# Value products for four units in a row with eight buffers of probabilities, and two steps between a copy and the product that needs it in both halves

## The chip, the cores and the metric

The kernel runs on one core of one Trainium2 chip. The metric is the device time of one launch in microseconds (us). The kernel before took 1185.13 us, the median of three runs (1181.31, 1185.13 and 1186.98).

## The reference

One decoder layer on 64 sequences of 128 tokens with 128 features: self-attention with 16 heads of width 8, cross-attention of the same form on 77 context tokens with a mask, and a mixture of 8 experts of which each token takes 2. In front of each stands a layer norm, behind each a residual sum.

```python
q = x @ Wq.T * (1.0 / sqrt(D));  k = x @ Wk.T;  v = x @ Wv.T          # (B, S, 16, 8) each
attn = softmax(einsum('bqhd,bkhd->bhqk', q, k));  out = einsum('bhqk,bkhd->bqhd', attn, v) @ Wff.T + bff
...
scores = einsum('bhqd,bhkd->bhqk', q, k) / sqrt(8);  scores = where(mask == 0, -1e9, scores)
...
gate_scores = einsum('bsd,ed->bse', l2norm(x @ Wp.T), l2norm(sim_matrix)) / temperature
top_v, top_i = top_k(gate_scores, 2);  comb = sum(one_hot(top_i, E) * softmax(top_v)[..., None], -2)
h = gelu(einsum('bsd,edf->ebsf', x, W1) + b1);  out = einsum('ebsd,bse->bsd', h @ W2 + b2, comb)
...
x = x + attn(layernorm(x));  x = x + xattn(layernorm(x), ctx);  x = x + ffn(layernorm(x))
```

## The kernel before, in words

The program has two phases. Phase A (to about 860 us) does both attentions, the gate and the sorting of tokens by expert. Phase B (from about 880 us) runs the experts over tiles of 512 tokens. The change lies in phase A alone.

Phase A works on blocks of four sequences, 16 in all. Its outer loop counts t from -3 to 19 (`steps`), and each engine has its own copy of the loop body. Each body has two halves. The x half attends block t ("s", self-attention) and at the same time forms the maxima for block t+1 ("m"). The y half attends the context for block t-2 ("c") and forms the maxima for block t-1 ("cm"). Everything else (transposes, projections, layer norms, the gate) belongs to blocks t-3 to t+3 and is hung between the units of these two halves.

One half has 16 units (one sequence, four heads) and 19 steps, u = 0 to 18. In step u TensorE does, in this order: `scores` of unit u (four products into one of two banks `sc_m`, in the y half also the mask's product), `shifted` of unit u-1 (the same products, less the maxima, into one of two banks `sc_a`), in some steps `values` (the products of probabilities and values), and then what `in_x` or `in_y` names for that step. Before `scores(u)` it waits for the maximum of unit u-2, before `shifted(u)` for the exponential of unit u-2, since each has two banks. VectorE takes the maximum of each unit (`maxima`, a reduction) and then what its own `in_x` or `in_y` names for the step. ScalarE takes the exponential of unit u-1 (`attend`) into `probs` and then what its tables name. All three engines work through their instructions in the order in which the code lists them.

`values` of one unit are four products of fp32 numbers with 32 columns of weights each, which stand beside each other in the array (`pv[...][VW * c:VW * (c + 1)]`). An fp32 product is two matmuls in the trace, so a unit has 8 of them. All other products have 128 or 77 columns of weights. Before, `values` of two units follow in steps 4, 6, 8, ... 18:

```python
if u >= LEAD + 2 and u % 2 == 0:
    values(n, b, u - LEAD - 3, va, last)
    values(n, b, u - LEAD - 2, va, last)
```

GpSimd splits maxima and remainders and issues the sorted stores. The Sync queue carries nearly all DMAs in the order of its code: in the y half it stores the split q, k and ck of the coming blocks (each waits for GpSimd), then loads `xin`, the x of block t+3, then stacks q and k. `stats("1", t + 3, xin)` on VectorE is the only reader that waits for this load; it starts the layer norm ("1") of block t+3, which ScalarE's `normalise` finishes in the next x half.

Of the kernel before, what the change touches and what calls it, by code (L numbers as in the profile page):

```python
# [33 lines left out]
NS = 4  # L34
# [33 lines left out]
NO = NS // 2  # L68

# [12 lines left out]
def program(nc, x, ctx_in, mask, Wq, Wk, Wv, Wff, bff, xWq, xbq, xWk, xbk, xWv, xbv, xWo, xbo,  # L82
            Wp, WpT, sim, temp, W1, b1, W2, b2, out):
    ctx = ExitStack()
    with ctx:
# [63 lines left out]
        xn = {n: sa(f"xn_{n}", [128, NS, D]) for n in ("1", "2")}  # L149
# [21 lines left out]
        probs = [sa(f"probs{i}", [128, T]) for i in range(4)]  # L171
# [126 lines left out]
        with nc.Block() as block:  # L298
# [277 lines left out]
            def _(act):  # L576
# [50 lines left out]
                def body(t, par):  # L627
                    def in_x(u):
# [13 lines left out]
                        if u == 8 and on_(t + 2):  # L642
                            evac(xnT["1"][:], "x1T", t + 2, 0)
                        if u == 9 and on_(t):
                            evac(cT[:], "cT", t, 1, TC)
                        if u == 10 and on_(t + 2):
                            first("q", t + 2)
                        if u == 11 and on_(t):
                            wait_block(act, dumped["ck"], t - 1)
                            first("ck", t, bk_c)  # L650
                        if u == 12 and on_(t + 2):
                            second("q", t + 2)
                        if u == 13 and on_(t + 2):
                            first("k", t + 2)
                        if u == 13 and on_(t):
                            second("ck", t)

                    def in_y(u):
# [12 lines left out]
                        if u in (8, 9) and on_(t - 3):  # L671
                            half = u - 8
# [10 lines left out]
                        if 10 <= u < 10 + NS and on_(t):  # L683
                            normalise("2", t, x2, u - 10)
# [30 lines left out]
            def _(dve):  # L715
# [68 lines left out]
                def choose(b):  # L784
# [8 lines left out]
                    for s in range(NS):  # L793
# [4 lines left out]
                        .then_inc(dv_ok.sem, 1)  # L798
                    for s in range(NS):
# [48 lines left out]
                def body(t, par):  # L848
                    def in_x(u):
                        if u < NO and on_(t - 3):  # L850
                            divide("c", t - 3, u)
                        if u == 6 and on_(t - 3):
                            wait_block(dve, x3_st, t - 4)
                            add_residual("c", t - 3, x2res[1 - par], x3)
                        if u == 7 and on_(t - 3):
                            stats("3", t - 3, x3)
                        if u == 11 and on_(t + 2):
                            wait_block(dve, part3["cq"], t - 1)
                            remainder("q", t + 2)
                        if u == 12 and on_(t):  # L860
                            wait_block(dve, part3["ck"], t - 1)
                            remainder("ck", t, bk_c)
                        if u == 14 and on_(t + 2):
# [710 lines left out]
```

## Time and profile before

| | |
|---|---|
| median of three runs | 1185.13 us (1181.31 to 1186.98) |
| the profiled execution | 1185.62 us, of which its span is 1183.9 us |
| PE busy | 996.1 us (84% of the span) |
| ACT, DVE, POOL busy | 799.0, 749.3, 593.3 us |
| granted TensorE clock, mean | 0.941 |

PE is TensorE's matmuls, PEld its weight loads, DVE is VectorE, ACT ScalarE, POOL GpSimd, SPq the Sync queue. A line of the timeline merges neighbouring instructions of one group: its first number is the start of the first, its second the time from there to the end of the last. Matmuls overlap in the trace, so what a group costs is the time from its start to the start of the next group, not its duration.

### The profile page before, as it was taken

To read this page: it belongs to the slowest core of one execution; us is meant where nothing else is said; L and a number is where in the kernel's file an instruction comes from. 1 tells how busy PE (TensorE), PEld (TensorE's weight loads), DVE (VectorE), ACT (ScalarE), POOL (GpSimd) and SP (SyncE) were. 2 spreads that over 40 slices of the span, in tenths; PEclk is the share of its full clock that TensorE was granted. 3 is DMA by queue.
4 is the path that set the end of the run, shared out by engine and by line. 5 is a ranking of instruction groups with operands and counts; after the bars stand their busy time and mean duration, and the time that the engine had idled before them with its cause. 6 is when DMAs were issued, how large, how long until landed. Compare 5 with 4: busy or idle time off the path is not lost. (4 is left out here: it accounts for less than half of the span.)

```text
span 1183.9 us, 31785 instructions
## 1 busy us (share of the span) xinstructions
PE 996.1 (84%) x11621; PEld 767.5 (65%) x11621; DVE 749.3 (63%) x2074; ACT 799.0 (67%) x1649; POOL 593.3 (50%) x821
## 2 busy tenths in 40 slices
PE   2567889999999999999999999847529999999940
PEld 1345667777777777777777777635418888888830
DVE  2554746666667666676666674423258888888836
ACT  2144557777777777777777777635419999999930
POOL 4313423365655664664654643544534666666650
PEclk9997999999999999999999999978759999999975
DMA  3337684455455555545545642230452444232319
GB/s 92 83 75 157 141 187 102 120 142 146 128 151 134 134 136 140 142 126 140 151 112 147 147 110 73 57 81 31 136 161 76 125 129 113 79 83 75 84 56 372
DMA packets 120387, 144.16 MB, mean 122 GB/s; under 512 B 34189, under 2 KB 98528, under 8 KB 115432
## 3 DMA queue, kind: packets, MB, share of 16 engines
q1 hardware_dynamic: 108888, 120.33, 40.0%
q0 software_dynamic: 9168, 17.21, 4.8%
q10 hardware_dynamic: 2176, 4.59, 1.0%
q8 instruction: 93, 1.52, 0.6%
q14 instruction: 62, 0.51, 0.1%
HBM read 88.38 MB, written 55.36 MB: 121 GB/s over the span
## 5 line engine op out<-in xcount | busy, mean ns | idle before, releaser
L615 ACT ACTIVATE probs<-sc_a 77x512 f32<-77x512 f32 (+1 forms) x512 | 301.0, 592 | 148.5 <-PE sc_a L1008 93.2
L757 DVE TENSOR_REDUCE negm_m<-sc_m 128x4 f32<-128x512 f32 x256 | 169.5, 683 | 82.5 <-PE sc_m L987 81.4
L1305 POOL DMA_INDIRECT y_d<-yo,row x156 | 160.7, 1030 | 115.0 <-DVE yo L1419 73.6
L757 DVE TENSOR_REDUCE negm_cm<-sc_m 128x4 f32<-128x308 f32 x256 | 119.1, 471 | 144.5 <-PE sc_m L992 143.0
L477 POOL DMA_INDIRECT xs_d<-xrow,slot_i x128 | 131.9, 1031 | 121.3 <-PE sc_a L1008 80.0
L1022 PE MATMUL pv<-probs,big 128*32 128x128 f32 x4096 | 165.7, 280 | 0.6
L987 PE MATMUL sc_m<-ks,qs 96*128 96x128 bf16 x1024 | 105.3, 230 | 37.5 <-DMA ks<-stk_k 13.4
L1022 PEld LDWEIGHTS pv<-probs,big 128*32 128x32 f32 x4096 | 96.3, 109 | 56.2 <-ACT probs L615 28.6
L1400 DVE TENSOR_TENSOR gl<-g,gh 128x512 fp32r<-128x512 f32 x156 | 107.4, 689 | 35.1 <-ACT g L1349 34.6
L987 PEld LDWEIGHTS sc_m<-ks,qs 96*128 96x128 bf16 x1024 | 71.6, 102 | 82.6 <-issue 55.8
L1003 PE MATMUL sc_a<-cqs,cks 102*77 102x128 bf16 x1024 | 102.0, 223 | 4.9 <-DMA cqs<-cmscr 4.8
L1003 PE MATMUL sc_a<-qs,ks 102*128 102x128 bf16 x1024 | 101.1, 223 | 1.2 <-ACT probs L615 1.2
L1008 PE MATMUL sc_a<-identb,mbias 128*77 128x512 bf16 x256 | 99.9, 390 | 0.0
L987 PE MATMUL sc_m<-cks,cqs 96*128 96x77 bf16 x1024 | 80.6, 202 | 20.9 <-DMA cqs<-cmscr 16.4
L1003 PEld LDWEIGHTS sc_a<-cqs,cks 102*77 102x77 bf16 x1024 | 89.1, 119 | 12.7 <-issue 6.0
L987 PEld LDWEIGHTS sc_m<-cks,cqs 96*128 96x128 bf16 x1024 | 65.5, 100 | 41.6 <-issue 27.3
L992 PE MATMUL sc_m<-mbias,identb 128*128 128x308 bf16 x256 | 78.7, 308 | 0.0
L1003 PEld LDWEIGHTS sc_a<-qs,ks 102*128 102x128 bf16 x1024 | 69.5, 99 | 5.1 <-ACT probs L615 2.5
L454 POOL TENSOR_TENSOR xres<-xagain,bff_b 128x512 f32<-128x512 f32 x16 | 20.4, 1272 | 96.5 <-DMA xagain<-x_dram 96.5
L1524 PE MATMUL pv<-gl,vh 128*128 128x512 f32 x156 | 64.7, 415 | 0.0
L1518 PE MATMUL pv<-gh,vh 128*128 128x512 f32 x156 | 62.4, 400 | 0.0
L1519 PE MATMUL pv<-gh,vl 128*128 128x512 f32 x156 | 61.8, 396 | 0.0
(202 smaller groups left out, 2333.7 us busy)
## 6 DMA issues: line engine op xcount, KB each, us to landing
xg<-xs_d SPq DMA_DIRECT2D x39, 260.0 KB
stk_q<-parts_q SPq DMA_DIRECT2D x16, 384.0 KB, 2.9
stk_k<-parts_k SPq DMA_DIRECT2D x16, 384.0 KB, 2.7
qs<-stk_q SPq DMA_DIRECT2D x16, 384.0 KB, 5.9
ks<-stk_k SPq DMA_DIRECT2D x32, 192.0 KB
stk_cq<-parts_cq SPq DMA_DIRECT2D x16, 384.0 KB, 2.9
cqs<-stk_cq SPq DMA_DIRECT2D x16, 384.0 KB
xin<-x_dram SPq DMA_DIRECT2D x16, 256.0 KB
```

Source lines behind the costliest of these rows:

```text
L477: nc.gpsimd.indirect_dma_start(out=xs_d, in_=xrow[b % 2][:, c // 2, c % 2, :], in_offset=None, out_offset=bass.IndirectOffsetOnAxis(ap=slo ...
L615: nc.scalar.activation(probs[e % 4][0:rows], sc_a[e % 2][0:rows], ACT.Exp, scale=scale)\
L757: nc.vector.tensor_reduce(out=negm[n][:, s, HG * g + 4 * half:HG * g + 4 * half + 4], in_=sc_m[u % 2][:, 0:4 * cols].rearrange("p (j k) -> ...
L987: i = nc.tensor.matmul(sc_m[u % 2][:, j * cols:(j + 1) * cols], qst[0:KR, 4 * half + j, s * S:(s + 1) * S], kst[0:KR, HG * g + 4 * half + ...
L992: i = nc.tensor.matmul(sc_m[u % 2][:, 0:4 * cols], identb[:], bias[:, s, :].unsqueeze(1).broadcast_to([128, 4, cols]), start=False, stop=T ...
L1003: i = nc.tensor.matmul(sc_a[u % 2][0:cols, j * S:(j + 1) * S], kst[:, HG * g + 4 * half + j, s * cols:(s + 1) * cols], qst[:, 4 * half + j ...
L1008: i = nc.tensor.matmul(sc_a[u % 2][0:cols, :], bias[:, s, :], identb[:].unsqueeze(1).broadcast_to([128, 4, S]), start=False, stop=True, sk ...
L1022: i = nc.tensor.matmul(pv[s // 2][VW * c:VW * (c + 1), slot * S:(slot + 1) * S], va[:, HG * s + 4 * half + c, g, :], probs[u % 4][:, c * S ...
L1305: nc.gpsimd.indirect_dma_start(out=y12_d, in_=yo[par][:, c, :], in_offset=None, bounds_check=2 * B * S - 1, oob_is_err=False, out_offset=b ...
L1400: nc.vector.tensor_tensor(out=gl[c][:], in0=g[c][:], in1=hi32(gh[c][:]), op=ALU.subtract).then_inc(gl_ok.sem, 1)
L1518: nc.tensor.matmul(o, vh[par][:, w], gh[c][:], start=(c == 0), stop=False)
L1524: nc.tensor.matmul(y_banks[par][:], vh[par][:, c * 128:(c + 1) * 128], gl[c][:], start=False, stop=(c == FC - 1)).then_inc(w2_done.sem, 1)
```

## The change

`values` now follow for four units in steps 6, 10, 14 and 18, and `probs` has eight buffers in place of four. To make room the layer norms "1" and "2" share one buffer `xn`. Many entries of the tables move by one step, so that two steps lie between a copy on ScalarE and the product that reads it. One entry moves further: `stats("1", t + 3, xin)` on VectorE goes from step 10 of the y half to step 5. The gate's `choose` is cut in two (`choose`, `point`).

```diff
+NP = 8
-        xn = {n: sa(f"xn_{n}", [128, NS, D]) for n in ("1", "2")}
+        xn = dict.fromkeys("12", sa("xn", [128, NS, D]))
-        probs = [sa(f"probs{i}", [128, T]) for i in range(4)]
+        probs = [sa(f"probs{i}", [128, T]) for i in range(NP)]
...
@@ ScalarE, attend @@
-                            if e >= 4:
-                                act.wait_ge(pv_ok[n].sem, pv_ok[n].val(b, e - 3))
-                            nc.scalar.activation(probs[e % 4][0:rows], sc_a[e % 2][0:rows], ACT.Exp, scale=scale)\
+                            if e >= NP:
+                                act.wait_ge(pv_ok[n].sem, pv_ok[n].val(b, e - NP + 1))
+                            nc.scalar.activation(probs[e % NP][0:rows], sc_a[e % 2][0:rows], ACT.Exp, scale=scale)\
@@ ScalarE, in_x: x1T 8 to 9, cT 9 to 10, q 10 to 11, ck 11 to 12, second q 12 to 13 @@
-                        if u == 13 and on_(t + 2):
+                        if u == 14 and on_(t + 2):
                             first("k", t + 2)
-                        if u == 13 and on_(t):
+                        if u == 14 and on_(t):
                             second("ck", t)
@@ ScalarE, in_y: the gate's copies 8, 9 to 9, 10; normalise "2" 10..13 to 11..14 @@
...
@@ VectorE, in_x: add_residual c 6 to 7, stats 3 7 to 8, remainders q, ck, k one later @@
@@ VectorE, in_y @@
-                        if u == 6 and on_(t):
+                        if u == 5 and on_(t + 3):
+                            dve.wait_ge(x_in.sem, x_in.val(t + 3))
+                            stats("1", t + 3, xin)
+                        if u == 7 and on_(t):
                             wait_block(dve, x2res_ok, t - 1)
                             add_residual("s", t, xres, x2)
-                        if u == 7 and on_(t):
+                        if u == 8 and on_(t):
                             stats("2", t, x2)
-                        if u == 10 and on_(t + 3):
-                            dve.wait_ge(x_in.sem, x_in.val(t + 3))
-                            stats("1", t + 3, xin)
                         if u == 12 and on_(t - 3):
                             choose(t - 3)
                         if u == 13 and on_(t - 3):
+                            point(t - 3)
+                        if u == 14 and on_(t - 3):
                             mark(t - 3)
...
@@ TensorE, values and beside @@
-                                             probs[u % 4][:, c * S:(c + 1) * S], start=(g == 0), stop=(g == 1))
+                                             probs[u % NP][:, c * S:(c + 1) * S], start=(g == 0), stop=(g == 1))
...
-                            if u >= LEAD + 2 and u % 2 == 0:
-                                values(n, b, u - LEAD - 3, va, last)
-                                values(n, b, u - LEAD - 2, va, last)
+                            if u >= 6 and u % 4 == 2:
+                                for v in range(u - 6, u - 2):
+                                    values(n, b, v, va, last)
@@ TensorE, in_x: project c 5 to 6, x1T, cT, q, ck one later @@
-                        if u == 13 and on_(t + 2):
+                        if u == 14 and on_(t + 2):
                             product("k", t + 2, w_k[:], xnT["1"][:], T)
@@ TensorE, in_y: project s 5 to 6, the gate's products 8, 9 to 9, 10, x2T, rank, cq one later @@
```

The order on TensorE from step 5 of the y half of a full block on, before. `pv<-probs` are the value products (line 1022), `sc_m` and `sc_a` those of `scores` and `shifted`, `w_ff` the projection and `third_m` the transposed maxima:

```order
L987 MATMUL sc_m<-cks,cqs 128x77 x4
L992 MATMUL sc_m<-mbias,identb 128x308
L1003 MATMUL sc_a<-cqs,cks 77x128 x4
L1008 MATMUL sc_a<-identb,mbias 77x512
L1022 MATMUL pv<-probs,big 32x128 x8
L1046 MATMUL wb<-identb,third_m 48x128 x4
```

And in the changed kernel, where the same places have the lines 993, 998, 1009, 1014, 1028, 983 and 1052:

```order
L993 MATMUL sc_m<-cks,cqs 128x77 x4
L998 MATMUL sc_m<-mbias,identb 128x308
L1009 MATMUL sc_a<-cqs,cks 77x128 x4
L1014 MATMUL sc_a<-identb,mbias 77x512
L1028 MATMUL pv<-probs,big 32x128 x16
L983 MATMUL wb<-w_ff,onT 128x128 x4
L1052 MATMUL wb<-identb,third_m 48x128 x4
```

The groups of value products are twice as long and half as many, and the projection has moved behind one of them.

The order on VectorE in the y half of the same block, before. `negm_cm` are the maxima, `lnst<-xin` is the layer norm of the load, `x<-wb,xres` the residual sum:

```order
L757 TENSOR_REDUCE negm_cm<-sc_m 128x4 x5
L780 TENSOR_TENSOR x<-wb,xres 128x512
L757 TENSOR_REDUCE negm_cm<-sc_m 128x4
L731 BN_STATS lnst<-x 128x6 x4
L736 BN_AGGR lnmv<-lnst 128x2 x4
L757 TENSOR_REDUCE negm_cm<-sc_m 128x4 x3
L731 BN_STATS lnst<-xin 128x6 x4
L736 BN_AGGR lnmv<-lnst 128x2 x4
L757 TENSOR_REDUCE negm_cm<-sc_m 128x4 x2
```

And in the changed kernel (lines 758, 732, 737 and 781):

```order
L758 TENSOR_REDUCE negm_cm<-sc_m 128x4 x4
L732 BN_STATS lnst<-xin 128x6 x4
L737 BN_AGGR lnmv<-lnst 128x2 x4
L758 TENSOR_REDUCE negm_cm<-sc_m 128x4 x2
L781 TENSOR_TENSOR x<-wb,xres 128x512
L758 TENSOR_REDUCE negm_cm<-sc_m 128x4
L732 BN_STATS lnst<-x 128x6 x4
L737 BN_AGGR lnmv<-lnst 128x2 x4
L758 TENSOR_REDUCE negm_cm<-sc_m 128x4 x4
```

The statistics of `xin` now stand behind the sixth reduction (two stand ahead of these rows), in front of the residual sum; they stood behind the eleventh.

The order on ScalarE at the end of the x half, before. `parts_k<-wb` copies the product k, `probs` are the exponentials:

```order
L597 ACTIVATE parts_q<-rest_q 128x512
L615 ACTIVATE probs<-sc_a 128x512
L590 ACTIVATE parts_k<-wb 128x512
L597 ACTIVATE parts_ck<-rest_ck 128x308
L615 ACTIVATE probs<-sc_a 128x512 x3
L625 ACTIVATE oT<-pv 128x512
```

And in the changed kernel (lines 598, 616, 591 and 626):

```order
L598 ACTIVATE parts_q<-rest_q 128x512
L616 ACTIVATE probs<-sc_a 128x512
L591 ACTIVATE parts_k<-wb 128x512
L598 ACTIVATE parts_ck<-rest_ck 128x308
L616 ACTIVATE probs<-sc_a 128x512 x2
L626 ACTIVATE oT<-pv 128x512
```

The copy of k now has two exponentials behind it in its half in place of three.

## Rows read from the trace of the kernel before

**Rows 1.** Stretches: us, busy (instructions) of PE PEld DVE ACT POOL, PEclk, DMA share, GB/s.

```profile
250.00:700.00 450.00, 437.65 (x6476) 335.51 (x6476) 298.57 (x942) 338.96 (x756) 260.22 (x398) 1.00 0.54 137
```

**Rows 2.** Waits of PE from 250 to 700 us: total, times, longest.

```profile
PE sc_m L987 <- DVE negm_m L757: 7.6, 11, 0.7
```

**Rows 3.** Timeline of PE, one x half (start, us, what): value groups and neighbours.

```profile
425.82 0.39 PE L1003 MATMUL sc_a<-qs,ks 102*128 102x128 bf16 x4
426.05 0.39 PE L987 MATMUL sc_m<-ks,qs 96*128 96x128 bf16 x4
...
432.26 0.39 PE L1003 MATMUL sc_a<-qs,ks 102*128 102x128 bf16 x4
432.57 0.64 PE L1022 MATMUL pv<-probs,big 128*32 128x128 f32 x16
433.15 0.40 PE L987 MATMUL sc_m<-ks,qs 96*128 96x128 bf16 x4
```

**Rows 4.** Timeline of PE cut at 426.9 us, which leaves 12 matmuls.

```profile
426.59 0.53 PE L1022 MATMUL pv<-probs,big 128*32 128x128 f32 x12
```

**Rows 5.** Timeline of PE, fourth step of the same x half.

```profile
419.36 0.40 PE L987 MATMUL sc_m<-ks,qs 96*128 96x128 bf16 x4 [0.70 <-DVE negm_m L757]
```

**Rows 6.** Timeline of DVE: reductions at that x half's start, statistics in the y half.

```profile
402.52 0.86 DVE L731 BATCH_NORM_STATS2 lnst<-x 128x6 f32<-128x128 f32 x4
...
403.78 0.45 DVE L757 TENSOR_REDUCE negm_cm<-sc_m 128x4 f32<-128x308 f32 x1
...
417.30 0.68 DVE L757 TENSOR_REDUCE negm_m<-sc_m 128x4 f32<-128x512 f32 x1
...
419.94 1.87 DVE L757 TENSOR_REDUCE negm_m<-sc_m 128x4 f32<-128x512 f32 x3
```

**Rows 7.** Timeline of PE, end of that x half.

```profile
434.52 0.39 PE L987 MATMUL sc_m<-ks,qs 96*128 96x128 bf16 x4
...
436.54 1.33 PE L1022 MATMUL pv<-probs,big 128*32 128x128 f32 x32
437.80 0.32 PE L987 MATMUL sc_m<-cks,cqs 96*128 96x77 bf16 x4
```

**Rows 8.** Timeline of ACT, the same stretch.

```profile
434.73 0.60 ACT L590 ACTIVATE parts_k<-wb 128x512 bf16<-128x512 f32 x1
...
435.57 1.82 ACT L615 ACTIVATE probs<-sc_a 128x512 f32<-128x512 f32 x3
```

**Rows 9.** Timeline of PE: starts of three y halves, and step 8 of one.

```profile
257.58 0.31 PE L987 MATMUL sc_m<-cks,cqs 96*128 96x77 bf16 x4
...
392.57 0.32 PE L987 MATMUL sc_m<-cks,cqs 96*128 96x77 bf16 x4
...
402.30 0.30 PE L987 MATMUL sc_m<-cks,cqs 96*128 96x77 bf16 x4
...
617.79 0.30 PE L987 MATMUL sc_m<-cks,cqs 96*128 96x77 bf16 x4
```

**Rows 10.** Timeline of the Sync queue: issues of the load of `xin`.

```profile
23.98 0.49 SPq L368 DMA_DIRECT2D xin<-x_dram  x1
...
263.10 0.66 SPq L368 DMA_DIRECT2D xin<-x_dram  x1
...
395.69 0.65 SPq L368 DMA_DIRECT2D xin<-x_dram  x1
...
622.43 1.68 SPq L368 DMA_DIRECT2D xin<-x_dram  x1
```

**Rows 11.** Timeline of DVE: a statistic that waited for `xin`.

```profile
28.51 0.87 DVE L731 BATCH_NORM_STATS2 lnst<-xin 128x6 f32<-128x128 f32 x4 [6.89 <-DMA xin<-x_dram]
```

**Rows 12.** DMA issues from 120 to 700 us: count, size, median us to landing.

```profile
xagain<-x_dram SPq DMA_DIRECT2D x13, 256.0 KB, 5.7
```

**Rows 13.** Timeline of PE: a wait of 2.33 us.

```profile
167.40 0.30 PE L987 MATMUL sc_m<-cks,cqs 96*128 96x77 bf16 x4 [2.33 <-issue]
```

**Rows 14.** Stretches behind that wait (columns as in rows 1).

```profile
168.00:171.00 3.00, 3.00 (x23) 2.54 (x22) 1.83 (x5) 0.59 (x1) 0.00 (x0) 0.50 0.99 248
```

More of the change, by code:

```diff
@@ L641, in in_x @@
                             evac(parts["cm"][:], "cm", t - 2, 0, rows=3 * H)
-                        if u == 8 and on_(t + 2):
+                        if u == 9 and on_(t + 2):
                             evac(xnT["1"][:], "x1T", t + 2, 0)
-                        if u == 9 and on_(t):
+                        if u == 10 and on_(t):
                             evac(cT[:], "cT", t, 1, TC)
-                        if u == 10 and on_(t + 2):
+                        if u == 11 and on_(t + 2):
                             first("q", t + 2)
-                        if u == 11 and on_(t):
+                        if u == 12 and on_(t):
                             wait_block(act, dumped["ck"], t - 1)
                             first("ck", t, bk_c)
-                        if u == 12 and on_(t + 2):
+                        if u == 13 and on_(t + 2):
                             second("q", t + 2)
-                        if u == 13 and on_(t + 2):
+                        if u == 14 and on_(t + 2):
                             first("k", t + 2)
-                        if u == 13 and on_(t):
+                        if u == 14 and on_(t):
                             second("ck", t)
@@ L670, in in_y @@
                             evac(parts["m"][:], "m", t + 1, 0, rows=3 * H)
-                        if u in (8, 9) and on_(t - 3):
-                            half = u - 8
+                        if u in (9, 10) and on_(t - 3):
+                            half = u - 9
                             n = f"pj{half}"
@@ L682, in in_y @@
                                 .then_inc(drained[n].sem, 1)
-                        if 10 <= u < 10 + NS and on_(t):
-                            normalise("2", t, x2, u - 10)
+                        if 11 <= u < 11 + NS and on_(t):
+                            normalise("2", t, x2, u - 11)
                         if u == 13 and on_(t + 2):
@@ L851, in in_x @@
                             divide("c", t - 3, u)
-                        if u == 6 and on_(t - 3):
+                        if u == 7 and on_(t - 3):
                             wait_block(dve, x3_st, t - 4)
                             add_residual("c", t - 3, x2res[1 - par], x3)
-                        if u == 7 and on_(t - 3):
+                        if u == 8 and on_(t - 3):
                             stats("3", t - 3, x3)
-                        if u == 11 and on_(t + 2):
+                        if u == 12 and on_(t + 2):
                             wait_block(dve, part3["cq"], t - 1)
                             remainder("q", t + 2)
-                        if u == 12 and on_(t):
+                        if u == 13 and on_(t):
                             wait_block(dve, part3["ck"], t - 1)
                             remainder("ck", t, bk_c)
-                        if u == 14 and on_(t + 2):
+                        if u == 15 and on_(t + 2):
                             wait_block(dve, part3["k"], t + 1)
@@ L1075, in in_x @@
                             by_token("cv", t - 1, 0, cT, cw_v[:], D, SC)
-                        if u == 5 and on_(t - 3):
+                        if u == 6 and on_(t - 3):
                             project("c", t - 3, cw_o)
@@ L1079, in in_x @@
                             maxima_T("cm", t - 2)
[L1080 removed]
+                        if u == 9 and on_(t + 2):
                             pe.wait_ge(ln_ok["1"].sem, ln_ok["1"].val(t + 2))
                             transposes("x1T", t + 2, 0, [xn["1"][:, s, :] for s in range(NS)], 128)
[L1083 removed]
+                        if u == 10 and on_(t):
                             pe.wait_ge(c_in.sem, c_in.val(t))
                             transposes("cT", t, 1, [cin[:, s, :] for s in range(NS)], 128)
[L1086 removed]
+                        if u == 11 and on_(t + 2):
                             pe.wait_ge(drained["x1T"].sem, drained["x1T"].val(t + 2))
                             product("q", t + 2, w_q[:], xnT["1"][:], T)
[L1089 removed]
+                        if u == 12 and on_(t):
                             pe.wait_ge(drained["cT"].sem, drained["cT"].val(t))
                             product("ck", t, cw_k[:], cT[:], TC)
[L1092 removed]
+                        if u == 14 and on_(t + 2):
                             product("k", t + 2, w_k[:], xnT["1"][:], T)
@@ L1102, in in_y @@
                             transposes("x3T", t - 3, 0, [xrow[(t - 3) % 2][:, s, 0, 0:D] for s in range(NS)], 128)
-                        if u == 5 and on_(t):
+                        if u == 6 and on_(t):
                             project("s", t, w_ff)
@@ L1106, in in_y @@
                             maxima_T("m", t + 1)
-                        if u in (8, 9) and on_(t - 3):
-                            half = u - 8
+                        if u in (9, 10) and on_(t - 3):
+                            half = u - 9
                             n = f"pj{half}"
@@ L1118, in in_y @@
                             by_token("v", t + 2, 0, xnT["1"], w_v[:], D, S)
-                        if u == 14 and on_(t):
+                        if u == 15 and on_(t):
                             pe.wait_ge(ln_ok["2"].sem, ln_ok["2"].val(t))
                             transposes("x2T", t, 1, [xn["2"][:, s, :] for s in range(NS)], 128)
-                        if u == 15 and on_(t - 3):
+                        if u == 16 and on_(t - 3):
                             claim(0, "rank", t - 3)
@@ L1134, in in_y @@
                             i.then_inc(filled["rank"].sem, 1)
-                        if u == 16 and on_(t):
+                        if u == 17 and on_(t):
                             pe.wait_ge(drained["x2T"].sem, drained["x2T"].val(t))
```

5 lines of the change are left out of this document (1 added, 4 removed).

## The prediction

> **What bounds the kernel now.** I read first where TensorE has idle time, since the change adds and removes no arithmetic. In a stretch of ten full blocks it is busy for 437.65 of 450 us at the full clock, 2.4 GHz (granted 1.00), and VectorE, ScalarE and GpSimd for 299, 339 and 260 us [rows 1]. So phase A's middle is TensorE's stream. What it still waits for there is small, most of it VectorE's maxima: 7.6 us in 11 waits [rows 2]. Overlapping matmuls hide short waits from these sums, so the timeline's starts decide. A full block (x half and y half) takes 45.0 us: the y halves that start at 257.58 and 617.79 are eight blocks apart [rows 9].
>
> **The value products.** With nothing in between, the four matmuls of `shifted` cost 0.23 us before the next `scores` (425.82 to 426.05). In front of value products the same four take 0.31 us, and the group of two units takes 0.58 us to its successor (432.57 to 433.15) [rows 3]. Four matmuls lengthen such a group by 0.11 us (0.53 us for 12, 0.64 for 16) [rows 4, 3], so one more unit, eight matmuls, costs 0.22. Two units would then be 0.44; the group's 0.58 holds 0.14 for getting in and out, and 0.08 to 0.09 more stand in front. A group that disappears saves 0.23 us.
>
> The Trainium skill has this as a rule: changing the array's tiling mode drains it (page TensorEngine Tiling (Array Packing), section Tiling Modes), and a drain is about 128 cycles (page TensorE: Matmul & The Clock Gate, section Step-by-step: what each phase is for). By these figures two drains would be an estimate of 0.11 us a group, half of what the rows show, and the saving below would be 12 us; the rows decide.
>
> Groups before: eight in a y half, seven in an x half, where those of steps 16 and 18 stand side by side. After: four each. Seven groups less a block, 7 x 0.23 = 1.64 us. Some 15 blocks run both attention and maxima in a half. Gross gain: 15 x 1.64 = 24.6 us.
>
> **Waits that the new order makes or ends inside a block.** Start of the x half: the first maximum there begins only at 417.30, behind the remainder of cq, and from it hangs the wait of 0.70 us at 419.36 [rows 6, 5]. Now 0.44 us more of value products lie between the cq product and the half's start, so the remainder is done that much sooner against it: -0.4. Middle of the x half, steps 7 to 9: these steps now have no value products, and TensorE needs 0.23 + 0.23 = 0.46 us for one [rows 3], VectorE (1.87 - 0.69) / 2 = 0.59 for its reduction, with the statistics (1.26 us from 402.52 to 403.78) and the residual sum (about another 0.6) behind two of them [rows 6]. With two banks `scores` of step 9 then waits about 0.26 us and of step 10 about 0.28, against 0.2 that is lost near there now: +0.3. End of the x half: ScalarE has the copy of k, a second copy and then the exponentials in a row; the copy starts 0.21 us behind the product (434.52, 434.73), the exponentials 0.84 later [rows 7, 8]. Product k moves from step 13 to 14, behind four units, so the two last exponentials follow the copies at once: the last is ready 1.05 (0.21 + 0.84) + 0.5 (about half of the 0.84 that two copies took, for the first exponential) + 0.65 (the duration of the last) = 2.2 us behind product k. TensorE reaches it after 0.46 + 0.23 + 0.08 + 3 x 0.22 = 1.4. A wait of 0.76 in place of the 0.25 that the last group has now (1.26 us from 436.54 to 437.80 in place of 1.01) [rows 7]: +0.5. In the y half ScalarE's normalisation of layer norm 2 and the copies around x2T and cq come close: +0.2. Sum +0.6, bounds 0 and 1.2. Net gain 1.04 a block, 15 x 1.04 = 16 us (6 to 25).
>
> Eight buffers of `probs` free each one earlier than it is asked for; the shared `xn` is written by ScalarE only after its own copies of the transposes, so both cost nothing. The other moved steps end small waits or none.
>
> **The wait that it adds.** `stats("1", t + 3, xin)` moves from step 10 of the y half to step 5, on VectorE directly behind the sixth maximum. Its load is issued in the same half, by a queue that first waits for GpSimd's splits. In the nine halves from 257.58 to 617.79 the issue comes 3.1 to 5.5 us behind the half's start (first 263.10 with 257.58, the third is the lowest, 395.69 with 392.57, last 622.43 with 617.79 [rows 9, 10]), mean 4.1. The time from issue to use: 4.5 us at 23.98, where VectorE did wait [rows 10, 11], and 5.7 for the load `xagain`, which is of the same size and from the same tensor [rows 12]. I take 5.1, between the two. So the data are there at +9.2 us (7.6 to 11.2), in every one of these halves later than VectorE comes to them (about +6).
>
> Behind the waiting instruction stand the seventh maximum and all that follows. TensorE needs the seventh (unit 6) for `scores` of step 8. Before, step 8 began at 402.30 - 392.57 = +9.73 [rows 9]; after, with one group less, at +9.47. The maximum is ready 1.26 + 0.48 + 0.1 = 1.9 us behind the landing, so TensorE stands for landing + 1.9 - 9.5 = 1.6 us (0 to 3.6). Nine such halves: 15 us (landing at 4.5: 10; at 5.7: 20). That is not covered by anything: steps 5 to 7 are the cover and I have counted them.
>
> The page TensorE: Matmul & The Clock Gate, section Architectural detail, says in its words that ACT and DVE are "strict FIFO". By that rule the maxima can't pass the statistic, which is the 15 us; with an engine that let them pass it would be 0. Rows 11 agree, as VectorE did nothing in those 6.89 us though later work was listed.
>
> **The clock.** After the wait of 2.33 us at 167.40 the clock was granted at 0.50 (1.2 GHz) from 168 to 171, with TensorE busy all the time [rows 13, 14]: some 1.5 us lost. I take two of the nine halves to be hit so: 3 us (0 to 14, where all are).
>
> **Sum** against the profiled execution, 1185.6 us with a span of 1183.9 and 1.7 around it: 1185.6 - 16 + 15 + 3 = 1187.6. The median of the runs lies 0.5 lower: 1187.
>
> **The rivals.**
> A, faster. The load lands soon enough: at 4.5 us behind the issue the stall is 10 us, without clock loss, and with waits at the low bound the net gain is up to 22: 1185 - 16 + 10 = 1179 with 16, 1173 with 22, and 1168 where the stall is half that; middle 1174. For it: the low end of the landing, +7.6, is just where TensorE's cover ends. Against it: the mean of the nine is 1.6 us behind that.
> B, slower. The stall is a little longer and the clock falls with it. The place is `scores` of step 8 in the y half; at 5.7 us from issue to landing the wait is 2.2 us, from about 2 us on (the 2.33 of rows 13) the clock goes down, at 1.5 us each: 1185 - 16 + 20 + 9 x 0.8 = 1196, at worst 1185 - 10 + 25 + 14 = 1214.
> C, slower: VectorE can't follow four steps in a row, and the 0.6 us a block of waits is 1.2 or more in both halves. Then 1187 + 9 = 1196. Against it: VectorE is busy in 299 of 450 us.
> D, the groups save nothing: the 0.23 us is paid for each unit and not for each group. Then 1187 + 25 = 1212. Against it: 12 matmuls and 16 differ by 0.11 only.
>
> **How the numbers follow.** The forecast, in which stall and gain cancel, has 0.38 (its own range 1179 to 1191); A 0.32, B 0.22, C 0.06, D 0.02. Within 0.5% is 1179.2 to 1191.1, which is about what a measurement of this kernel can tell from no change. Faster 0.32 (A), same 0.38, slower 0.30 (B, C, D). The range 1171 to 1200 leaves out the far ends of A and of B, C, D.
>
> **What would show it.** Value groups of 32 matmuls in four places a half that cost about 1.01 us to their successor; a y half without a stall some 0.7 us shorter. Idle time of VectorE before the statistics on `xin`, ended by its load, some 3 us in each of nine halves, about 30 in all; behind it TensorE waiting for `negm_cm` some 15 us in sum, in step 8. At the x half's end a wait of about 0.8 us for `probs` inside the last group. Stretches of granted 0.50 in y halves where none are now. If VectorE doesn't wait for `xin`, A holds and I am wrong about the load; if the full blocks without a stall are not about 44 us long, I am wrong about the groups.

## The result and the profile after

The changed kernel takes 1195.37 us, the median of six runs (1190.60 to 1196.56); the kernel before, run beside it, 1183.18 us (1179.25 to 1186.98). The ratio is 1.0095, 95% interval 1.0067 to 1.0124: slower, inside the range, but not the forecast. Measured a second time, beside three of the experiments below, it was 1.0073 (1.0047 to 1.0098).

| profiled execution | before | after |
|---|---|---|
| time, span | 1185.62, 1183.9 us | 1196.27, 1194.5 us |
| PE busy | 996.1 us | 987.4 us |
| DVE waits for `xin` | 12.2 us in 2 | 44.2 us in 13 |
| mean granted clock | 0.941 | 0.927 |
| a pair of halves without a stall | 45.0 us | 44.4 us |

TensorE is busy for 9 us less and the kernel takes 11 more. In the stretch of [rows 1] the busy time fell from 437.65 to 427.63 us and the granted clock from 1.00 to 0.99:

```profile
250.00:700.00 450.00, 427.63 (x6364) 337.77 (x6362) 293.44 (x931) 333.69 (x747) 256.13 (x390) 0.99 0.53 134
```

The waits of TensorE there, against [rows 2] (total, times, longest); the first is new, the second fell from 7.6 us and is part of the gain:

```profile
PE sc_m L993 <- DVE negm_cm L758: 9.2, 5, 2.5
PE sc_m L993 <- DVE negm_m L758: 3.8, 9, 0.4
PE pv L1028 <- ACT probs L616: 2.8, 10, 0.3
PE wb L972 <- DVE on L771: 1.7, 9, 0.2
PE wb L977 <- ACT xnT L584: 1.7, 10, 0.2
```

One stalled y half, which starts at 354.85, in the timelines of three engines (start, length, what, wait). The Sync queue issues the load 4.05 us behind the half's start, as in [rows 10]:

```profile
358.43 0.43 SPq L310 DMA_DIRECT2D stk_ck<-parts_ck  x1
358.90 0.66 SPq L369 DMA_DIRECT2D xin<-x_dram  x1
```

VectorE stands for it 4.20 us, and only then takes the two maxima behind it:

```profile
360.51 0.48 DVE L758 TENSOR_REDUCE negm_cm<-sc_m 128x4 f32<-128x308 f32 x1 [0.95 <-PE sc_m L998]
365.19 0.87 DVE L732 BATCH_NORM_STATS2 lnst<-xin 128x6 f32<-128x128 f32 x4 [4.20 <-DMA xin<-x_dram]
366.16 0.38 DVE L737 BATCH_NORM_AGGREGATE lnmv<-lnst 128x2 f32<-128x6 f32 x4
366.46 0.83 DVE L758 TENSOR_REDUCE negm_cm<-sc_m 128x4 f32<-128x308 f32 x2
```

TensorE waits at the `scores` of step 8, where the half before stood at 402.30 without one [rows 9]:

```profile
366.96 0.32 PE L993 MATMUL sc_m<-cks,cqs 96*128 96x77 bf16 x4 [2.05 <-DVE negm_cm L758]
```

In the stretch of 3.4 us behind it (columns as in rows 1) it is busy all the time at half the clock, 1.2 in place of 2.4 GHz:

```profile
364.00:367.80 3.80, 1.75 (x26) 1.26 (x24) 2.51 (x11) 1.07 (x2) 0.00 (x0) 1.00 0.99 228
367.80:371.20 3.40, 3.40 (x25) 2.74 (x22) 2.56 (x12) 1.89 (x7) 1.28 (x3) 0.51 0.55 131
```

This half took 27.2 us against 23.4 of one without a stall, 3.8 more. Its step 8 starts 12.11 us behind the half's start, where that of a half without a stall starts at 9.91 (448.37 and 458.28 below). So 2.2 us went ahead of step 8 (the idle record shows 2.05 of them), and the other 1.6 behind it, where the clock was at half. The nine y halves of the middle took 27.56, 23.54, 27.16, 24.15, 23.38, 25.86, 23.37, 23.36 and 26.99 us, 15.1 us over nine times 23.36. Five show a wait of TensorE (2.48, 2.05, 0.56, 2.25, 1.87), and three of these (2.48, 2.05, 1.87) are followed by 3.41 us at 0.50. By the starts of step 8 the nine lost 10.1 us ahead of it, and the rest of the 15.1, 5.0, nearly all in the three stretches at half the clock. In the profile of the second measurement the same nine halves are 13.0 us over nine times 23.36, with one wait of 4.23 us in the first of them.

Where nothing stalls the change does gain. A half in which VectorE waited for the load too (1.92 us), but not so long that TensorE did, and the half behind it:

```profile
448.37 0.31 PE L993 MATMUL sc_m<-cks,cqs 96*128 96x77 bf16 x4
...
455.10 1.08 PE L1028 MATMUL pv<-probs,big 128*32 128x128 f32 x32
456.12 1.16 PE L983 MATMUL wb<-w_ff,onT 128*128 128x128 f32 x8
...
458.28 0.30 PE L993 MATMUL sc_m<-cks,cqs 96*128 96x77 bf16 x4
...
469.70 1.10 PE L977 MATMUL wb<-xnT,cw_q 128*128 128x512 f32 x2 [0.16 <-ACT xnT L584]
...
471.74 0.40 PE L993 MATMUL sc_m<-ks,qs 96*128 96x128 bf16 x4
...
490.96 0.64 PE L1028 MATMUL pv<-probs,big 128*32 128x128 f32 x16
491.88 0.91 PE L1028 MATMUL pv<-probs,big 128*32 128x128 f32 x16 [0.28 <-ACT probs L616]
492.73 0.32 PE L993 MATMUL sc_m<-cks,cqs 96*128 96x77 bf16 x4
```

The y half is 471.74 - 448.37 = 23.37 us (23.74 before), the x half 20.99 (21.25). Groups of 32 cost 1.02 us (455.10 to 456.12), and the last one 1.77 (490.96 to 492.73) against 1.26 in [rows 7].

The account of the span, +10.6 us: the start of block 3's x half 196.35 in place of 191.35, +5.0; from there to the start of block 14's (686.51 before), eleven blocks, -7.1 by the gain and +15.1 by the stall; the rest -2.5.

### The profile page after: what moved, and what is told of

It reads as the page before. It is cut to its first block and busy times, and to the rows that moved or that the text cites. A ratio compares the mean times of both kernels' runs of the same rounds, so it can differ in the third digit from the quotient of the medians.

```text
span 1194.5 us, 31657 instructions
## 1 busy us (share of the span) xinstructions
PE 987.4 (83%) x11621; PEld 780.0 (65%) x11621; DVE 750.2 (63%) x2074; ACT 796.0 (67%) x1649; POOL 593.0 (50%) x821
## 5 line engine op out<-in xcount | busy, mean ns | idle before, releaser
L1028 PE MATMUL pv<-probs,big 128*32 128x128 f32 x4096 | 145.3, 277 | 4.9 <-ACT probs L616 3.9
L1028 PEld LDWEIGHTS pv<-probs,big 128*32 128x32 f32 x4096 | 102.5, 110 | 43.1 <-ACT probs L616 30.8
L428 POOL TENSOR_SCALAR lnve<-lnmv 128x4 f32<-128x4 f32 x48 | 11.6, 241 | 129.8 <-DVE lnmv L737 127.7
```

The costliest lines, as they stand in the source:

```text
L1028: i = nc.tensor.matmul(pv[s // 2][VW * c:VW * (c + 1), slot * S:(slot + 1) * S], va[:, HG * s + 4 * half + c, g, :], probs[u % NP][:, c * ...
```

## The experiments

Ratios are to the kernel before, run beside it on the same chip. "A pair" is an x half and a y half of full blocks, from TensorE's first `scores` to the next x half's; where a mean of nine is given, some of the nine are stalled.

| kernel | ratio (95%) | a pair, us |
|---|---|---|
| changed kernel | 1.0095 (1.0067 to 1.0124) | 44.4, mean of nine 46.1 |
| only statistics moved | 1.0114 (1.0092 to 1.0135) | 45.0, mean of nine 47.1 |
| statistics back | 0.9925 (0.9904 to 0.9947) | 44.36 |
| load issued early | 0.9950 (0.9933 to 0.9967) | 44.35 |
| groups of four only | 1.0040 (1.0022 to 1.0057) | 45.6 to 46.4, mean of nine 46.0 |
| moves by one step only | 1.0165 (1.0141 to 1.0189) | 46.25 |
| values one by one | 1.0261 (1.0236 to 1.0285) | 47.4 |
| k back | 0.9925 (0.9906 to 0.9945) | 44.27 |
| y waits | 0.9940 (0.9922 to 0.9958) | 44.46 |
| copy sooner | 0.9846 (0.9825 to 0.9867) | 43.71 |
| values last | 0.9916 (0.9896 to 0.9936) | 44.31 |

**The statistics back in step 10.**

```diff
-                        if u == 5 and on_(t + 3):
+                        if u == 10 and on_(t + 3):     # behind stats("2")
                             dve.wait_ge(x_in.sem, x_in.val(t + 3))
                             stats("1", t + 3, xin)
```

> The changed kernel, in which only the statistics of xin stand again in step 10 of the y half, as in the kernel before. Theory (the load of xin stops VectorE and with it TensorE): the five long y halves of 27.6, 27.2, 24.2, 25.9 and 27.0 us shrink to the 23.4 of the others, 15 us less, the three stretches of granted clock 0.50 in the blocks' middle go with them, and TensorE starts block 3's x half where it did before (191 us and not 196), 5 less: about 1175 us, or 0.992 to 0.995 of the kernel before, since the gain of 0.64 us a block stays. VectorE's idle time ahead of the statistics on xin falls from 44 us in 13 waits to the 12 in 2 of before. Rival (the groups of four and the bursts of maxima cost what was lost): it stays at 1195, 1.009 of before, and the y halves stay long.

Measured: 0.9925, 1184.43 us against 1192.96. All nine y halves take 23.34 to 23.60 us and no stretch at 0.50 lies in the middle. The wait for `xin` in this kernel and in the changed one:

```profile
DVE lnst L732 <- DMA xin<-x_dram: 13.2, 2, 7.2
```

```profile
DVE lnst L732 <- DMA xin<-x_dram: 44.2, 13, 7.2
```

So this one entry turned 0.7% of gain into 1% of loss. Only the start did not follow: block 3's x half began at 195.3 us in this profile.

**Only the statistics moved**, the same line alone in the kernel before.

> The kernel before, in which only the statistics of xin are moved, from step 10 to step 5 of the y half, ahead of the residual sum. Theory: the same stall as in the changed kernel, 15 us in the full blocks and some 5 at the start, perhaps a little less since step 8 begins 0.3 us later here: 1198 to 1204 us, 1.013 to 1.018 of before. Rival (the wait is harmless by itself and needs the new order around it): 1183, ratio 1.000.

Measured: 1.0114, just below the expected 1.013, but clearly slower. The profile shows the stall with nothing else changed; in the y half that starts at 261.39 TensorE's wait is the longest seen, 4.34 us (the changed kernel's longest is 2.48 in its first profile and 4.23 in its second, in the same place), and the granted clock behind it 0.50:

```profile
275.63 0.44 PE L987 MATMUL sc_m<-cks,cqs 96*128 96x77 bf16 x4 [4.34 <-DVE negm_cm L757]
```

```profile
276.00:281.00 5.00, 5.00 (x39) 3.80 (x38) 2.64 (x12) 1.49 (x7) 1.71 (x4) 0.50 0.42 98
```

That half took 30.86 us in place of 23.75; all halves of the middle together some 19 us more than before. The rival, that the wait needs the new order around it, is out.

**The load issued early**, statistics left in step 5.

```diff
+                    if on_(t + 3):
+                        wait_block(sp, ln_ok["1"], t + 2)
+                        sp.dma_start(xin[:], x_v[t + 3]).then_inc(x_in.sem, 16)
                     if on_(t + 2):
                         dump("q", t + 2)
                         dump("k", t + 2)
...
-                    if on_(t + 3):
-                        wait_block(sp, ln_ok["1"], t + 2)
-                        sp.dma_start(xin[:], x_v[t + 3]).then_inc(x_in.sem, 16)
```

> The changed kernel with the statistics left at step 5, in which the Sync queue issues the load of xin as its first work of the y half, ahead of the stores of the split q and k, which wait for GpSimd. Theory (the landing time alone makes the stall): the load is issued 3 to 5 us sooner and is there before VectorE asks, so the y halves are 23.4 us as with the statistics at step 10, and the time is that of the kernel with them there, 0.992 of before, 0.983 of the changed kernel. Rival (the statistics' 1.26 us between the sixth and seventh maximum are the cost, or the transfer only lands later where it is issued sooner, behind others): as the changed kernel, 1.009 of before.

Measured: 0.9950; its interval overlaps that of the statistics put back. The queue issues the load 3.7 us ahead of the half's start (256.07), in the nine halves on average 4.2 ahead of it in place of 4.1 behind it: 8 us sooner, where 3 to 5 were expected. VectorE comes to it 6.1 us behind the half's start and has nothing to wait for:

```profile
252.39 0.51 SPq L361 DMA_DIRECT2D xin<-x_dram  x1
```

```profile
262.14 0.86 DVE L732 BATCH_NORM_STATS2 lnst<-xin 128x6 f32<-128x128 f32 x4
```

This separates the two halves of the mechanism: the early statistics cost nothing by their own 1.26 us, only by the load's landing behind them. Eight of the nine y halves take 23.36 us, one 23.62. How little of the 8 us would have been enough isn't shown. The Trainium skill's rule (page TensorE: Matmul & The Clock Gate, section Architectural detail), that VectorE is strictly in order, is what ties the two together, and these three runs agree with it: putting the statistics back took some 18 to 20 us off (from 1.0073 or 1.0095 to 0.9925), moving them alone added 13, issuing the load early took 15 off (1193.01 to 1177.81 on one chip).

**Groups of four only.** `NP = 8`, the shared `xn` and the new condition for `values`; every other step as before.

```diff
-                            if u >= LEAD + 2 and u % 2 == 0:
-                                values(n, b, u - LEAD - 3, va, last)
-                                values(n, b, u - LEAD - 2, va, last)
+                            if u >= 6 and u % 4 == 2:
+                                for v in range(u - 6, u - 2):
+                                    values(n, b, v, va, last)
```

> The kernel before with only the value products in groups of four units, eight buffers of probabilities and the one xn buffer; every entry of the tables keeps its step. Theory (0.23 us for each of seven groups in a block, less waits that the burst makes): unstalled pairs of halves of 43.9 to 44.4 us in place of 45.0, so 9 to 16 us less, 1167 to 1174 us, 0.986 to 0.993 of before. Rival 1 (the moves by one step are what makes room, without them the burst costs what it saves): 45.0 us a pair, 1.000. Rival 2 (the moves by one step cost the waits that I priced): more than 1.2 us a pair gained here, below 1167.

Measured: 1.0040, outside all three. Rival 1 is the nearest, and it doesn't go far enough. TensorE's timeline of one pair, its waits and what stands in front of them:

```profile
278.58 0.40 PE L988 MATMUL sc_m<-ks,qs 96*128 96x128 bf16 x4
...
284.79 1.13 PE L978 MATMUL wb<-cw_o,onT 128*128 128x128 f32 x8 [0.31 <-ACT onT L584]
...
289.52 0.63 PE L967 MATMUL wb<-ident,xn 128*128 128x128 f32 x4 [0.80 <-ACT parts_m L584]
...
311.08 0.70 PE L1115 MATMUL wb<-wpx,xnT 128*128 128x136 f32 x4 [0.53 <-ACT parts_m L584]
...
322.17 1.10 PE L972 MATMUL wb<-xnT,cw_q 128*128 128x512 f32 x2 [0.60 <-ACT xnT L584]
...
324.21 0.40 PE L988 MATMUL sc_m<-ks,qs 96*128 96x128 bf16 x4
```

All four waits are for copies on ScalarE. I read them so: while TensorE works off 32 matmuls it hands ScalarE nothing; then come two steps without value products, ScalarE has exponentials and copies at once, and TensorE is at the next product before its copy is done. 0.31 + 0.80 + 0.53 + 0.60 = 2.24 us of waits stand against the 1.64 that seven groups give back, and 324.21 - 278.58 = 45.63 us is 0.6 more than before. That the two numbers differ by just 0.6 is partly chance, since the idle records miss a part of each wait and some waits of before ended; the sign doesn't hang on it. This pair is one of the shortest: the mean of nine is 46.0 us, 1.0 over that of before, and the start (187.0 us to block 3's x half, 4 sooner than before) hides some of it in the ratio.

**The moves by one step only**, that is the kernel with the statistics back and value products in twos.

> The kernel with the statistics back at step 10, and with the value products in groups of two as before the change, so that of the change only the moves by one step are left. Theory (the moves save little by themselves, they make room for the groups of four): a pair of halves 44.9 to 45.2 us, 1.000 of before. Rival (the moves bring the gain of the changed order and the groups nothing): 44.4 us, 0.9925 as with groups of four.

Measured: 1.0165. Both theories are wrong: the moves by themselves cost 1.25 us a pair. The pair from 333.49 on takes 46.24:

```profile
333.49 0.40 PE L993 MATMUL sc_m<-ks,qs 96*128 96x128 bf16 x4
...
336.53 0.40 PE L993 MATMUL sc_m<-ks,qs 96*128 96x128 bf16 x4 [0.70 <-DVE negm_m L758]
...
347.25 0.40 PE L993 MATMUL sc_m<-ks,qs 96*128 96x128 bf16 x4 [0.22 <-DVE negm_m L758]
...
354.58 0.91 PE L1028 MATMUL pv<-probs,big 128*32 128x128 f32 x16 [0.27 <-ACT probs L616]
```

The first of these waits is there before, too [rows 5]. By the starts of the two timelines, the cost lies in the transposes of the context `cin` with the wait behind them at 347.25 (0.4 us), the two projections (0.3), the x half's last group (1.76 us in place of 1.26) and the place ahead of the y half's transposes of layer norm 2, where TensorE waits 0.28 us for ScalarE's normalisation and starts 0.4 us later; some other groups give 0.4 back.

With the moved entries, groups of four are worth 46.25 - 44.36 = 1.89 us a pair (I had priced 1.64), and with the entries where they were they cost 0.6 or more. So the change's two halves can't be judged alone: one is +0.4%, the other +1.65%, both together -0.75%.

**Values one by one.**

```diff
-                            if u >= LEAD + 2 and u % 2 == 0:
-                                values(n, b, u - LEAD - 3, va, last)
-                                values(n, b, u - LEAD - 2, va, last)
+                            if u >= 4:
+                                values(n, b, u - 4, va, last)
+                            if u == 18:
+                                values(n, b, 15, va, last)
```

> The kernel before with the value products of one unit in each step (4 to 18, two units in the last) in place of two in every second. It has 7 groups more in a y half and 7 more in an x half, 14 in a block. Theory (0.23 us for each group, for getting in and out of the products with 32 columns): 14 x 0.23 x 15 blocks = 48 us more, about 1231 us, 1.04 of before; in the timeline a group of 8 matmuls costs 0.36 us to its successor. Rival (the price is paid for each unit): no change, 1183.

Measured: 1.0261, 31 us and not 48. The price of a group is as expected, as the timeline shows: 0.31 us in front, 0.36 to the next `scores`.

```profile
379.86 0.42 PE L1022 MATMUL pv<-probs,big 128*32 128x128 f32 x8
380.22 0.32 PE L987 MATMUL sc_m<-cks,cqs 96*128 96x77 bf16 x4
...
380.74 0.38 PE L1008 MATMUL sc_a<-identb,mbias 128*77 128x512 bf16 x1
381.05 0.42 PE L1022 MATMUL pv<-probs,big 128*32 128x128 f32 x8
```

Groups of 8, 16 and 32 cost 0.36, 0.58 and 1.01 us (medians): 0.22 for a unit, 0.14 for getting in and out, and 0.31 - 0.22 = 0.09 in front. The count was wrong: nothing lies between the values of the last steps, so there are 12 groups more and not 14, and 12 x 0.23 = 2.8 us a pair, of which 2.4 arrived, since one wait inside a group became shorter. D is out. By the Trainium skill (page TensorEngine Tiling (Array Packing), section Tiling Modes, for the drain, and page TensorE: Matmul & The Clock Gate, section Step-by-step: what each phase is for, for its 128 cycles) 0.11 us a group was the estimate, half of the 0.23 measured.

**Product k back in step 13**, with its copies and its remainder one step sooner too, on top of the statistics back.

```diff
-                        if u == 14 and on_(t + 2):
+                        if u == 13 and on_(t + 2):
                             product("k", t + 2, w_k[:], xnT["1"][:], T)
```

> The changed kernel with the statistics of xin at step 10 again and with the product k, its two copies and the copy of the second part of ck in step 13 and its remainder in step 14, as before the change, so that three exponentials and not two follow the copies before the last group. Theory: the x half's last group costs 1.26 us or less in place of 1.77 and the x half 20.5 in place of 21.0; 0.5 us x 15 blocks = 7 us, 0.994 of the kernel with the statistics back, 0.986 of before. Rival (TensorE waits for k's place elsewhere, since the values of step 14 then stand behind the product): 0.992 of before, no change by it.

Measured: 0.9925, a pair 44.27 against 44.36: the gain is 0.08 us and not 0.5. The last group did shorten, from 1.77 to 1.38 us (431.32 to 432.70), but `product` k, a step sooner, now starts 0.52 us behind the four matmuls ahead of it and not 0.22. It writes the bank that held the product q, and the last reader of that bank is VectorE's remainder of q, which ends at 427.97 behind a maximum; so the rival, a wait for k's place, holds:

```profile
427.50 0.39 PE L1009 MATMUL sc_a<-qs,ks 102*128 102x128 bf16 x4
428.02 1.12 PE L977 MATMUL wb<-xnT,w_k 128*128 128x512 f32 x2
...
431.32 1.45 PE L1028 MATMUL pv<-probs,big 128*32 128x128 f32 x32
432.70 0.32 PE L993 MATMUL sc_m<-cks,cqs 96*128 96x77 bf16 x4
```

```profile
427.29 0.68 DVE L746 TENSOR_TENSOR rest_q<-wb,parts_q 128x512 f32<-128x512 f32 x1
```

**The waits of the y half.** On top of that: transposes of layer norm 3 in step 5 and their copy in 6 (they were in 4 and 5), `normalise("2")` in 10 to 13 (11 to 14), the transposes `x2T` in 14 (15).

> As the kernel with k back, and in the y half the transposes of layer norm 3 in step 5 and their copy in step 6, the normalisation of layer norm 2 in steps 10 to 13 and its transposes in step 14, so that two steps lie between their copy and the product cq. Theory: the y half loses the waits of 0.2 us ahead of the transposes of xrow and of 0.3 us ahead of cq, 23.36 to about 22.9 us, 7 us in 15 blocks: 0.980 of before. Rival (ScalarE is as late as TensorE there, and the waits only move to the exponentials): 0.986 of before, as without it.

Measured: 0.9940; the y half 23.55 us, longer than 23.36. The wait of 0.2 us ahead of the transposes of `xrow` went, and that ahead of cq grew. ScalarE's timeline tells why: its copy `xnT` (455.94) stands behind an exponential, for whose input ScalarE stands idle for 0.92 us, while the transposes had been issued at 454.02.

```profile
454.31 0.22 ACT L695 ACTIVATE ev<-dv 128x4 f32<-128x4 f32 x1
455.45 0.59 ACT L616 ACTIVATE probs<-sc_a 77x512 f32<-77x512 f32 x1 [0.92 <-PE sc_a L1014]
455.94 0.58 ACT L584 ACTIVATE xnT<-wb 128x512 f32<-128x512 f32 x1
```

```profile
456.67 1.10 PE L977 MATMUL wb<-xnT,cw_q 128*128 128x512 f32 x2 [0.63 <-ACT xnT L584]
```

**The copy sooner.**

```diff
-                        if u == 15 and on_(t):
+                        if u == 14 and on_(t):
                             evac(xnT["2"][:], "x2T", t, 1)
```

> As the kernel with the y half's waits attacked, and ScalarE copies the transposed layer norm 2 at the end of step 14 and no longer of step 15. There the copy stood behind the exponential of unit 14, for which ScalarE waited 0.92 us with the transposes long done. Theory (the wait of 0.63 us ahead of cq is ScalarE's order): the copy is done 0.8 us sooner, the wait goes, and the y half takes 22.9 to 23.0 us in place of 23.55 (23.36 with layer norm 2 at its places of the changed kernel): 0.986 to 0.988 of before. Rival (the copy then holds up the exponential and values of the last units wait): 23.3 or more, 0.992.

Measured: 0.9846, 1163.83 us against 1182.45: the fastest version, 2.3% below the changed kernel by the ratios (0.9846 / 1.0073). ScalarE copies at 448.19, in the gap where it stood idle, and cq follows without a wait; the y half is 22.80 us.

```profile
448.19 0.60 ACT L584 ACTIVATE xnT<-wb 128x512 f32<-128x512 f32 x1 [0.18 <-PE wb L972]
448.92 1.08 ACT L616 ACTIVATE probs<-sc_a 77x512 f32<-77x512 f32 x2
```

```profile
449.27 0.24 PE L1138 MATMUL wb<-chosen,ones 128*128 128x8 bf16 x4
449.37 1.10 PE L977 MATMUL wb<-xnT,cw_q 128*128 128x512 f32 x2
```

**Values last in their step**, on top of the copy sooner.

```diff
-                            if u >= 6 and u % 4 == 2:
-                                for v in range(u - 6, u - 2):
-                                    values(n, b, v, va, last)
                         between(u)
+                        if attn:
+                            if u >= 6 and u % 4 == 2:
+                                for v in range(u - 6, u - 2):
+                                    values(n, b, v, va, last)
```

> As the kernel whose copy of layer norm 2 comes sooner (0.9846 of before), with each group of four units' value products behind what the table names for the step and no longer in front of it. Theory (a product of fp32 numbers with the full array costs more directly behind value products: the projection took 1.09 us there and 0.89 to 0.95 elsewhere, the gate's product 0.57 and 0.50): 0.3 to 0.5 us a block less, and copies get the group as cover; 43.3 us a pair in place of 43.7, 0.979 to 0.982 of before. Rival (these products then wait for their copies, 1 us sooner than now, and the first of them for VectorE's division): 43.7 us or more, 0.985 and up.

Measured: 0.9916; the rival held. The products came before their copies and banks, and the projection takes 1.05 us in front of a group as well, once the wait behind it is taken off (306.21 to 307.54 less 0.28). That it was dear for standing behind value products was wrong. In both orders the transposed maxima follow the projection directly, where before `scores` did (0.89 us); whether that is the reason isn't shown.

```profile
306.21 1.05 PE L983 MATMUL wb<-w_ff,onT 128*128 128x128 f32 x8
307.54 0.40 PE L1053 MATMUL wb<-identb,third_m 128*48 128x128 bf16 x4 [0.28 <-ACT xnT L584]
```

**The kernel before, profiled again.**

> The kernel before itself, for a second profile: its pairs of halves take 45.0 us again, and the start of block 3's x half (191.35 us in the first profile) shows how far the start-up differs between executions. If it is within 1 us of that, the 5 us that the changed kernel lost there belong to the change; if it differs by 3 or more, they can't be told from chance.

Measured: one time, 1180.49 us; pairs of 45.0 us, and block 3's x half at 190.38 us.

## Why the likeliest case failed and the range held

**The group switch, 0.23 us.** Right in price (0.14 inside a group and 0.09 in front, and 12 groups more cost 2.4 us) and in number (seven a block): 1.89 us a block where the table leaves room, against 1.64 priced. The 0.25 between them are waits, which I can't lay out one by one.

**Waits inside a block, +0.6.** The term of the sum that was furthest off for each block. With groups and moves in place the net gain is 45.0 - 44.36 = 0.64 us and not 1.04. The x half was close: -0.26 where 3 x 0.23 = 0.69 less the net 0.4 of waits gives -0.3, and the last group waited as worked out (+0.51). The y half was not: I gave its waits 0.2 us by a sentence on ScalarE, with no row behind it, and they are 4 x 0.23 - 0.38 = 0.54: 0.2 ahead of the transposes of `xrow`, 0.3 ahead of cq, 0.2 in the projection (1.09 us in place of 0.89), less some that ended. The first two show in the copy sooner, which takes 0.56 us out of the half by exactly these.

**"The other moved steps end small waits or none."** Wrong, and put at nothing without a row behind it. The moves cost 1.25 us a block where the groups are of two and save 1.3 (45.6 - 44.36, at the least) where they are of four. I had priced neither, since I looked for waits of before that the moves would end; the waits that they prevent exist only in the new order.

**The wait for `xin`.** Right in mechanism and place; the size was half as much again as measured. Issue 4.07 us behind the half's start (priced 4.1; of the nine issues of before the lowest is the fourth and not the third, and their mean is 4.0), data used at +9.0 on average (9.2), 6.9 to 10.8 in the single halves (7.6 to 11.2), VectorE's idle time for it 25.8 us in the nine halves (30 all told). TensorE's own wait was smaller, 10.1 us and not 15 (9.2 in the five idle records): step 8 comes 9.91 us behind the start and not 9.47, because of the y half's waits above, and starts 1.77 us behind the statistics (365.19 to 366.96) and not 1.9, so it is held up only by landings later than +8.1.

**The clock, 3 us.** Right in price (1.5 us a stretch; 1.6 measured) and too low in number, three halves and not two: 15.1 - 10.1 = 5.0 us, nearly all of it theirs. Stall and clock together were priced at 18 and came to 15.1.

**The start.** I priced nothing there; the profile lost 5.0 us before block 3's x half. The three executions with statistics ahead of the load (changed kernel 196.4 and 193.9, only statistics moved 195.2) are late, but so are two without (195.3 statistics back, 194.7 moves only), and the others, but for the values one by one (199.3), lie between 187.0 and 191.6. The two profiles of the kernel before differ by 0.97 us there, so by the measure set down before the second one the 5 us would belong to the change; but with the statistics put back they are still there (195.3), so it isn't the stall alone. Part of the 5 us may be chance; this stays open.

**The sum.** Forecast -16 + 15 + 3 = +2; profile -7.1 + 15.1 + 5.0 - 2.5 = +10.5. The last two numbers of the profile are what lies outside the eleven blocks, gain included. Counted over the whole kernel the gain is at most 7.1 + 2.5 = 9.6 in place of 16, stall and clock are 15.1 in place of 18, and the start adds 5.0 that had no term. So the missing 9 us are the gain and the start, and not the stall. The range held by its width. Rival B had the right sign and time (1196), but that is luck: its stall of 20 and clock loss of 7 came to 10.1 and 5.0, and a smaller gain and the start filled the gap. A fell with the landings, D with the price of the groups. C had the smaller gain right, and nearly its size (a pair 0.4 us above the forecast, where C says 0.6 or more); its cause, a VectorE that can't follow, shows only in the 3.8 us that TensorE still waits for `negm_m`.

## What to carry to other kernels

On an engine that takes its work in order, move a reader of a load only together with the load's issue: the line that did harm here was free once its transfer was issued first. Batching work on the busiest engine is worth its switches only when the copies and products between the batches are moved with it; each half measured alone looked like a loss. For the wait that is left, read the timeline of the engine that it names: where that engine itself is idle with another instruction at its head, exchanging the two is worth more than more distance (0.9940 to 0.9846 here).

## What was unexpected of the hardware

- The granted clock fell to 0.50 for 3.41 us behind waits of 2.48, 2.05 and 1.87 us of TensorE, but not behind one of 2.25 at 505.06. Each of the three stretches cost about 1.6 us, so a wait near 2 us may cost nearly as much again. In the second profile of the changed kernel it fell behind waits of 4.23 and 2.22 us, and not behind one of 1.24.
- The same 256 KB load, issued from the same place, was used 3.7 us behind its issue in one half (452.75 to 456.44) and 6.4 in another (632.01 to 638.45), VectorE waiting for it both times. From issue to use the busy share of the DMA engines was 1.0 or more in all nine halves, against 0.53 over the ten blocks, so the load always lands among other transfers; what makes it land sooner or later isn't shown.
